# Product-key expert kernel on one core: the first head's expert lookup in three pieces, and the lookups of the later heads dealt one behind the other

## The reference

```python
q = einsum('bnd,de->bne', layernorm(x), w_q)                  # 512 -> 2 halves * 8 heads * 128
q = (q - mean(q, (0,1))) * rsqrt(var(q, (0,1)) + eps) * gamma + beta
sim = einsum('pbnhd,hkpd->pbnhk', q, keys)                    # 2 halves, 8 heads, 128 keys
sx, ix = top_k(sim[0], 8);  sy, iy = top_k(sim[1], 8)
scores, pk = top_k(sx[..., :, None] + sy[..., None, :], 8)    # best 8 of 64 pairs
idx = take(ix * 128 + iy, pk)                                 # 8 experts per token and head
h = gelu(einsum('bnd,bnhkd->bnhk', layernorm(x), down[idx])) * softmax(scores)
out = x + einsum('bnhk,bnhkd->bnd', h, up[idx])
```

## Time and profile before

| quantity | value |
|---|---|
| median of 3 runs | 2746.43 us (2737.4 to 2747.01) |
| the profiled execution | 2732.75 us, span 2730.9 us |
| PE, DVE, ACT, POOL busy | 86%, 68%, 43%, 42% of the span |
| rows fetched by POOL's queue | 469.82 MB |
| mean granted TensorE clock | 0.943 |

### The profile page before, as it was taken

How to read it: one execution, slowest core, us unless ns; L and a number is a source line. 1 busy time by engine, 2 the same in 40 slices (tenths; PEclk the granted TensorE clock), 3 DMA queues, 4 the chain that set the end, 5 groups by cost and what they waited for, 6 DMA issues and landing times.

```text
span 2730.9 us, 37792 instructions
## 1 busy us (share of the span) xinstructions
PE 2356.3 (86%) x12444; PEld 1259.1 (46%) x12444; DVE 1869.2 (68%) x5474; ACT 1176.5 (43%) x3224; POOL 1144.1 (42%) x1082
## 2 busy tenths in 40 slices
PE   8999999999999999998868888778878788876767
PEld 4565555656555565655534433333333343332323
DVE  4676777777687777768467767677775766766554
ACT  3365574736557473657223423323333332332222
POOL 3111212111121211120166576676667666577665
PEclk9999999999999999999989999989899998898889
DMA  4001001010100101011189899999999999899998
GB/s 175 30 1 37 8 8 37 1 44 1 41 4 10 36 1 43 1 60 58 58 320 364 299 369 357 349 354 345 358 352 363 351 362 358 309 359 356 355 375 330
DMA packets 161954, 521.78 MB, mean 191 GB/s; under 512 B 17248, under 2 KB 27488, under 8 KB 161760
## 3 DMA queue, kind: packets, MB, share of 16 engines
q0 software_dynamic: 129024, 469.82, 45.8%
q1 hardware_dynamic: 31152, 48.03, 5.3%
q10 hardware_dynamic: 1584, 1.52, 0.2%
HBM read 508.30 MB, written 11.01 MB: 190 GB/s over the span
## 4 chain that ended last, share of the span: by engine, by line
PE 20%; issue 10%; DVE 10%; another core or an unknown queue 3%; POOL 3%; DMA 3%; ACT 1%; DVEq 1%; POOLq 0%; ACTq 0%
PE ps_y L1819 7%; PE ps_o L1819 7%; DVE e_rows L1965 5%; PE ps_s L1789 3%; POOL e_rows L1769 3%; DMA e_rows<-in_experts,e_idx 3%; PE ps_t L1802 1%; ACT e_diag L2047 1%; DVE acc L1955 1%; DVE e_at L1899 1%; DVE e_best_at L1879 1%; DVEq L1903 0%; DVE q_stats L1847 0%; ACT e_q_t L2022 0%
## 5 line engine op out<-in xcount | busy, mean ns | idle before, releaser
L1769 POOL DMA_INDIRECT e_rows<-in_experts,e_idx x896 | 908.6, 1014 | 473.0 <-issue 284.6
L1965 DVE CUSTOM_DVE_ANT_0 e_rows<-e_rows,xn_all 128x512 f32<-128x512 f32 x896 | 568.6, 688 | 148.4 <-DMA e_rows<-in_experts,e_idx 112.5
L1819 PE MATMUL ps_o<-e_rows,e_diag 128*128 128x512 f32 x896 | 443.1, 642 | 149.2 <-issue 131.3
L1819 PE MATMUL ps_y<-e_rows,e_diag 128*128 128x512 f32 x896 | 434.5, 632 | 121.6 <-ACT e_diag L2047 60.4
L2047 ACT ACTIVATE e_diag<-ident_f,e_weight 128x128 f32<-128x128 f32 x896 | 286.3, 390 | 560.5 <-DVE e_weight L1976 197.1
L1819 PEld LDWEIGHTS ps_o<-e_rows,e_diag 128*128 128x128 f32 x896 | 179.8, 206 | 384.7 <-issue 362.5
L1819 PEld LDWEIGHTS ps_y<-e_rows,e_diag 128*128 128x128 f32 x896 | 178.1, 203 | 355.1 <-issue 316.1
L1133 DVE SCALAR_TENSOR_TENSOR ring<-ps_s,mask 112x750 f32<-112x750 f32 x248 | 225.0, 936 | 129.2 <-PE ps_s L624 110.1
L1359 ACT ACTIVATE ring<-ring,neg_max 112x750 f32<-112x750 f32 x248 | 226.8, 916 | 157.6 <-DVE neg_max L1143 157.2
L1143 DVE CUSTOM_DVE_ANT_0 ring<-ring,mask_bias 112x750 f32<-112x750 f32 x248 | 233.5, 989 | 0.0
L2042 ACT ACTIVATE e_active<-e_hidden 128x4 f32<-128x4 f32 x224 | 45.6, 204 | 359.5 <-DVE e_hidden L1965 143.3
(11 more groups left out here) (226 smaller groups left out, 3189.8 us busy)
## 6 DMA issues: line engine op xcount, KB each, us to landing
e_rows<-in_experts,e_idx POOLq DMA_INDIRECT x896
xn_t<-in_ctx_t SPq DMA_DIRECT2D x8, 1500.0 KB, 6.7
w_in<-in_ffn_wq SPq DMA_DIRECT2D x16, 256.0 KB, 7.6
acc<-in_x SPq DMA_DIRECT2D x8, 448.0 KB, 4.9
acc<-x_dram SPq DMA_DIRECT2D x7, 512.0 KB, 6.5
xn_all<-x2n_dram SPq DMA_DIRECT2D x7, 512.0 KB, 7.1
out<-acc SPq DMA_DIRECT2D x14, 256.0 KB
x_dram<-x SPq DMA_DIRECT2D x7, 448.0 KB, 3.1
```

Source lines behind the costliest of these rows:

```text
L1769: pool.indirect_dma_start(rows[:, v % RING, k, :], None, table[:, :], bass.IndirectOffsetOnAxis(ap=idx[:, e:e + 1], axis=0))\
L1819: mm = nc.tensor.matmul(ps_out[t % 2][:], diag[:, HU * (v % ND) + k, :], rows[:, v % RING, k, D:], start=(s == 0 and k == 0), stop=(s == S ...
L1965: last = nc.vector.tensor_tensor_reduce(down, down, xn_all[:, t, :], 1.0, 0.0, ALU.mult, ALU.add, hidden[:, b, k:k + 1])
```

## The change

1. **Seam.** The last transposes of the attention write to `cross_bank(last, t)` (ps_y, ps_o) in place of `ps_t[t]`. The freed `ps_t[0]` takes a new `second_project`: the first column of head 0, half 1, on TensorE between `turn_last(1)` and `first_project(3, ...)`.
2. **Head 0 in `first_head`.** The other three columns of half 1 go first, then all seven matches of half 0, which now write to the four `ps_q` banks and wait for no search, then only the three first matches of half 1. Half 1's query uses the banks ps_m[0], ps_m[1], ps_out[0], ps_out[1]. ScalarE's `affine` waits per column for the matches that read the part of `q_t` it overwrites. The projections of head 1 no longer stand here.
3. **Three pieces** (0, 2), (2, 6), (6, 14). The first two are searched, paired and chosen ahead of the units. The last one, eight tiles, goes into steps of the units 0 to 5 (`REST_PE`, `REST_DVE`, `REST_ACT`, `FIRST_REST`).
4. **Dealing.** The steps of head 1 go two per unit into the units 1 to 20 of head 0. Those of each later head go evenly, 40 steps over 28 units, from v = 21 of the head two before to v = 20 of the head before. No two heads' steps overlap any more.

```diff
+            def second_project():
+
+                pe.wait_ge(act_ready.sem, act_ready.at(last, 3 * NT))
+                for kc in range(KC):
+                    mm = nc.tensor.matmul(ps_t[0][:, 0:QN], w_in[:, (KC + kc) * P:(KC + kc + 1) * P], xn_t[:, kc, 0:QN],
+                                          start=(kc == 0), stop=(kc == KC - 1))
+                mm.then_inc(second_q_done, 1)
...
             turn_last(1)
+            second_project()
             first_project(3, 0)
...
-FIRST_TILES = 2
-PIECES = ((0, FIRST_TILES), (FIRST_TILES, NTF))
+PIECES = ((0, 2), (2, 6), (6, NTF))
...
             if head == 0 and half == 1:
-                return (ps_out[0], ps_out[1], ps_q[0], ps_q[1])[c]
+                return (ps_m[0], ps_m[1], ps_out[0], ps_out[1])[c]
...
+        def sims_out(head, half, g):
+
+            if head == 0 and half == 0:
+                return ps_q[g // 2][:, (g % 2) * TPB * NK:(g % 2 + 1) * TPB * NK]
+            return ps_m[g % 2][:, 0:TPB * NK]
...
-        LEAD = 20
-        AHEAD = 2 * QC
-        FIRST_TURNS = [0, *(min(N_STEPS, AHEAD + 2 + 3 * v // 2) for v in range(NV))]
-        SECOND_TURNS = [0, 1, 2, 3, 4, 5, 6, 7, 8, 10, 12, 13, 14, 15, 16, 17, 18, 20]
-        SECOND_AT = NV - len(SECOND_TURNS) + 1
+        LAST_AT = 20
+
+        REST = PIECES[-1]
+        REST_PE = {0: [("match", 1, 3), ("match", 1, 4)], 3: [("match", 1, 5), ("match", 1, 6)]}
+        REST_DVE = {0: [("search", 0, 3), ("search", 0, 4)], 1: [("search", 0, 5), ("search", 0, 6)],
+                    2: [("search", 1, 3), ("search", 1, 4)], 3: [("search", 1, 5), ("search", 1, 6)],
+                    4: [("pairs", 0, 0), ("pairs", 0, 1)], 5: [("pairs", 0, 2), ("pairs", 0, 3)],
+                    6: [("choice", 0, 0), ("choice", 0, 1)], 7: [("choice", 0, 2), ("choice", 0, 3), ("choice", 0, 4)]}
+        REST_ACT = {5: [("soften", 0, 0)]}
+        FIRST_REST = ((0,), (1,), (2,), (3,), (4, 5), (6, 7))
...
+        START_AT = 1
+
+        def unit_of(head, k):
+
+            if head == 1:
+                return START_AT + k // 2
+            return NV * (head - 1) - (NV - LAST_AT) + 1 + k * NV // N_STEPS
...
         def steps_in(h, v):
...
+            return DEAL.get(NV * h + v, ())
...
             def first_head():
 
-                group_at = {1: (0, 1), 2: (2, 3), 3: (4, 5, 6)}
-                for c in range(QC):
-                    for part in range(2):
-                        project(0, 1, 2 * c + part)
-                    for g in group_at.get(c, ()):
-                        match_keys(0, 0, g)
-                ahead_at = {2: (0, 1, 2, 3, 4), 4: (5,), 5: (6,), 6: (7,)}
+                for i in range(2, 2 * QC):
+                    project(0, 1, i)
                 for g in range(NG):
+                    match_keys(0, 0, g)
+                for g in range(REST[0] // TPB):
                     match_keys(0, 1, g)
-                    for i in ahead_at.get(g, ()):
-                        project(1, 0, i)
...
-                for g in range(NG):
-                    search(0, 0, g)
-                    if 1 <= g <= QC:
-                        count(0, 1, g - 1)
+                for c in range(QC):
+                    count(0, 1, c)
                 affine(0, 1)
                 dve.wait_ge(iota_ready, 1)
-                done = 0
-                for n0, n1 in PIECES:
-                    for g in range(done, n1 // TPB):
-                        search(0, 1, g)
-                    done = n1 // TPB
+                for n0, n1 in PIECES[:-1]:
+                    for half in range(2):
+                        for g in range(n0 // TPB, n1 // TPB):
+                            search(0, half, g)
...
-                if n >= 1:
-                    act.wait_ge(sims_made, NG * n)
                 for c in range(QC):
+                    if n >= 1:
+                        act.wait_ge(sims_made, NG * (n - 1) + min(NG, -(-QN * (c + 1) // (P * TPB))))
```

More of the change, by code:

```diff
@@ L1435, in last_cross @@
                     n = last * S + t * TT
-                    nc.scalar.copy(xn_t[:, :, n:n + TT], ps_t[t][:, 0:KC * TT].rearrange("p (c n) -> p c n", c=KC))\
+                    nc.scalar.copy(xn_t[:, :, n:n + TT], cross_bank(last, t)[:, 0:KC * TT].rearrange("p (c n) -> p c n", c=KC))\
                         .then_inc(last_t_ready, 1)
@@ L1642, in q_bank, with sims_needed, first_searched @@
             if head == 0 and half == 1:
-                return (ps_out[0], ps_out[1], ps_q[0], ps_q[1])[c]
+                return (ps_m[0], ps_m[1], ps_out[0], ps_out[1])[c]
             return ps_q[c]
+        def sims_out(head, half, g):
+            if head == 0 and half == 0:
+                return ps_q[g // 2][:, (g % 2) * TPB * NK:(g % 2 + 1) * TPB * NK]
+            return ps_m[g % 2][:, 0:TPB * NK]
+        def sims_needed(head, half, g):
+            if head == 0 and half == 0:
+                return min(g // 2 * 2 + 2, NG)
+            return NG * nth(head, half) + g + 1
+        FIRST_SEARCHES = [(half, g) for n0, n1 in PIECES for half in range(2) for g in range(n0 // TPB, n1 // TPB)]
+        def first_searched(half, g):
+            return FIRST_SEARCHES.index((half, g)) + 1
         def piece_of(n0, n1):
@@ L1806, in steps @@
             def steps(head, k):
-                for stage, half, part in PE_STEPS.get(k, ()):
-                    if head == 1 and k < AHEAD:
-                        continue
+                for stage, half, part in steps_of(PE_STEPS, REST_PE, head, k):
                     (project if stage == "project" else match_keys)(head, half, part)
@@ L1937, in steps @@
             def steps(head, k):
-                for stage, half, part in DVE_STEPS.get(k, ()):
+                n0, n1 = REST if head == 0 else (0, NTF)
+                for stage, half, part in steps_of(DVE_STEPS, REST_DVE, head, k):
                     if stage == "count":
@@ L1945, in steps @@
                     elif stage == "pairs":
-                        pairs(head, part)
+                        pairs(head, part, n0, n1)
                     else:
-                        choice(head, part)
+                        choice(head, part, n0, n1)
             def add_rows(h, t):
```

62 lines of the change are left out of this document (32 added, 30 removed).

## The result

The changed kernel takes 2783.72 us (median of 4 runs, 2775.65 to 2790.21) against 2743.36 us: a ratio of 1.0148, 95% interval 1.0113 to 1.0183. It is slower by 40 us: less than 2%, but clear of the noise, and outside the range of the prediction (2700 to 2757). The profiled execution is the one of 2775.65 us, 42.9 us above that of before.

What follows compares the result with a forecast made beforehand. The prediction took the gather's transfers to bound the expert part. Gains of 5.2 (first index), 8.4 (hole) and 4 us (end of head 0), dealing 0, sum to 17.6 us; subtracted from the median, 2729 us, range 2700 to 2757.

Steps and rivals of the forecast that it cites:

- that is the pace of the gather: Head 7: its units, 5.70 us each at a DMA share of 0.97, were taken to show the gather's pace.
- rival 4: Start: first index comes no earlier and a new wait replaces the hole; 2746 us, chance 0.06.
- Seam and first index: Start: expert part begins 2.4 us later, yet head 0's first gather comes 5.2 us earlier, at 1353.0.
- The hole: Head 0's start: POOL's 12.37 us wait for the second piece's indices goes, regaining 8.4 us of transfer.
- Is it too thin?: Head 0, units 0 to 10: DMA starves about 2 us, ring reserve gone some 40 us; 3 us charged.
- rival 2: Head 0: two steps per unit and one 10 us stall leave 4 us of the gain; 2743 us, chance 0.20.
- The end of head 0: Head 0's last stretch, DMA share 0.70 for 40 us: 7 of 12 us regained, 4 us net after a charge.
- Dealing 0: Heads 1 to 6: the even deal changes nothing, 0 us; bounds 24 us gained or 32 us lost.
- rival 3: Pairs and choice, squeezed into fewer units, cost 4.5 us more in each of seven heads; 2761 us, chance 0.14.

Runs made afterwards that it cites:

- before_again: The kernel before, unchanged, run again for its trace; ratio 1.0008 to the kernel before.
- changed_third: The changed kernel, unchanged, run once more in one session with its parts; ratio 1.0054 to the kernel before.
- changed_again: The changed kernel, unchanged, run once more; ratio 1.0116 to the kernel before.
- pieces_alone: The kernel before with head 0's tiles in three pieces, all ahead of the units, nothing else moved; ratio 1.0021 to the kernel before.
- seam_only: The changed kernel with the third piece's lookup and head 1's projections ahead of the units, and the old deal; ratio 1.0004 to the kernel before.
- choice_spread: The kernel before with heads 2 to 7 dealt evenly, but pairs and choice one step per unit (v = 13 to 20); ratio 1.0067 to the kernel before.
- deal_alone_again: The kernel before with only the steps of heads 2 to 7 dealt evenly, 40 over 28 units; ratio 1.0046 to the kernel before.
- projects_ahead: The changed kernel with the old deal from head 3 on and head 1's eight projections of half 0 ahead of the units; ratio 0.9993 to the kernel before.

## Why the prediction was wrong, point by point

The step that failed is the first one, "that is the pace of the gather", read from the DMA share of 0.97 in head 7, with what it put at nothing on that strength: engine work inside the units. It gave the even deal 0, and head 0's extra steps 2 us of starved DMA and a charge of 3. Measured in the result: 29.8 us in heads 1 to 6 and 2.0 in head 7, and a head 0 that is 35.2 us longer, against units that begin 27.9 us earlier.

At level A half the bytes change nothing and a quarter fewer issues give 140 us, so heads 1 to 6 go near the pace of POOL's issues (112 x 1.30 = 146 us a head, measured 148 to 150) and head 0 near TensorE's. The prediction had the number in hand, 1.27 us from issue to issue, and set it aside as "under the 1.43 us a gather takes", a figure that was itself only head 7's time divided by its issues. A high DMA share did not tell which of the two was the bound. That the result was slower had been given a chance of 0.14. (In that sum, half of rival 4's 0.06 stands under "faster", although its 2746 is no change.)

Neither half the bytes nor fewer issues were tried at level B, and there heads of 166 to 172 us are not at the pace of the issues either. The timeline of POOL reads: in before 832 of the 895 steps from one issue's start to the next are of 2 us or less and sum to 1101.0 us, and 63 longer ones to 255.2; in after 810 sum to 1063.9 and 85 to 337.1. (At level A before_again has 22 longer ones with 61.2 us, changed_third 32 with 99.8.) So the 42.9 us of span are: first issue -7.3, issues' steps -37.1 + 81.9 = +44.8, and 5.4 behind the last issue. The loss is in POOL's long waits, most of them for TensorE to free a ring unit, and not in slower issues.

*Seam and first index: right.* Forecast 1353.0, measured 1350.95, 1354.31 (changed_again) and 1351.47 (changed_third): against 1358.23 (before), 1358.28 (pieces_alone, set 2) and 1358.96 (before_again): 4 to 7.5 us earlier.

*The hole: it closes, and another opens.* The 8.4 us were counted as transfer regained. Without a wait for an index the ring of six units is full after 24 issues, and POOL waits for the engines instead: 9.13 us at unit 7 in after, 22.56 us at unit 6 in pieces_alone, 10.87 us at unit 6 in seam_only. Neither of those two runs beats the kernel before. Rows that come earlier wait in the ring for engines that are not ready for them. That a closed hole is worth nothing in every order of the lookup is not shown: in pieces_alone the units also begin 9.5 us later.

*"Is it too thin?": right sign, size wrong.* I charged 2 us and a share of 3. TensorE inside head 0 carries the projections that stood ahead of the units before (8 x 1.50 = 12 us), in the time that the "hole" had given it for nothing, and it was at 141 of 147.8 us already. Units 1 to 5 also carry steps of head 0 and of head 1 side by side, so the change's description, that no two heads' steps overlap any more, is true only of the later heads. At level A head 0 takes 172.1 us in the changed kernel against 147.8, and begins 22.2 us earlier: head 1 starts 2.1 us later. TensorE is busy for 9.6 us more in it and VectorE for 9.8, so some 15 of the 24.3 us are time in which TensorE stands. At level B it takes 198.5 us against 163.3, and 16.6 us of that are the longer step from unit 0 to unit 1. Its signs were the ones that the prediction had named for rival 2, a POOL wait of over 5 us in units 6 to 16 (9.13 and 5.93).

*"The end of head 0": wrong.* The window of 0.70 is still there, 0.72 with TensorE busy for 41.70 of 46.50 us: the stretch was mostly TensorE's. That steps moved elsewhere in the same head cannot shorten it is argued.

*Dealing 0: wrong; rival 3 was nearest.* At level A it costs 0.46%, 12 us or 2 us a head. In the result heads 1 to 7 take 31.8 us more, and rival 3 had 32. That this agrees so closely is partly luck: rival 3 put the cost down to the density of pairs and choice, and choice_spread, which spreads them, is still 17 us slower than before. The windows of v = 15 to 18, 18 to 20 and 20 to 24 of head 4, of before_again and then of deal_alone_again, show where:

```profile
2064.41:2083.04 18.63, 13.52 (x27) 5.18 (x25) 17.40 (x47) 10.08 (x21) 14.66 (x14) 0.91 1.00 381
2083.04:2090.21 7.17, 6.15 (x14) 2.69 (x15) 6.70 (x24) 5.31 (x14) 5.65 (x6) 1.00 1.02 389
2090.21:2111.31 21.10, 21.10 (x64) 10.73 (x63) 15.37 (x59) 5.93 (x20) 16.03 (x17) 1.00 1.02 402
```

```profile
2068.20:2089.48 21.28, 14.28 (x29) 5.77 (x27) 18.86 (x81) 7.32 (x18) 16.71 (x16) 0.90 1.03 409
2089.48:2098.48 9.00, 8.28 (x13) 3.67 (x14) 8.67 (x26) 2.97 (x10) 6.90 (x7) 0.65 1.01 384
2098.48:2117.01 18.53, 18.53 (x46) 8.55 (x45) 12.79 (x41) 5.93 (x20) 14.23 (x15) 1.00 1.01 398
```

v = 15 to 20 take 30.3 us in place of 25.8 (29.3 to 31.1 in heads 1 to 6, against 25.6 to 26.1). The even deal puts two parts of pairs or choice into one unit twice, and those two steps from weights to weights take 8.7 and 8.5 us on average, against 6.8 and 6.0; 2.6 of the 4.5 us come back in the third row. In v = 18 to 20 (second row) TensorE is granted 0.65 of its clock here and 0.81 in most heads, where the old deal has 0.76 in three heads and 1.00 in three. Which share is the clock's and which VectorE's was not measured by itself. Two readings speak against taking this stretch for the whole cost. With half the bytes it is as long (29.2 to 30.8 us against 26.2 to 27.4), and yet heads 1 to 6 lose nothing. And in choice_spread three of six heads have it at 24.5 to 24.7 us, with a clock of 1.00 in v = 18 to 20 of all six, and the kernel is slower all the same. How the even deal costs its time stays open.

*What level B adds.* There VectorE has 33 idle times of 4 us or more in the expert part of each kernel, 191.6 us in before and 220.6 in after; at level A 2 (before_again) and 4 (changed_third). Rival 2's "one stall of 10 us" is this, and it was two stalls of 8.94 and 6.67 us at the point where the ring could not help. What stops the engines there was not shown. No operand was late; ScalarE, too, begins unit 1's gelu after 7.17 us for which the profile shows no cause, while TensorE works on until 1378.2 and only then waits, for ScalarE. The runs with half the gather fell on level A, which has none of these stops. That the engines lack instructions while the gathers fill the queues is argued only.

The Trainium skill, "SBUF — State Buffer", section "SBUF: two separate sides", says that GpSimd cannot write the descriptors of its DMAs while VectorE runs an instruction in a mode that takes the port pair they share. The issues do not show it: one takes 1.014 us on average in before and 1.007 in after (0.999 in before_again, 1.000 in changed_third), so the moved lookup did not slow them. Whether the lookup's instructions run in such a mode no run shows.

## What to carry to other kernels

A DMA share near 1.0 does not say that transfers set the pace. Look at the engine that issues them too, whose busy row leaves out the gap between two issues, and multiply the issues by the step from start to start (896 x 1.30 us here). Work taken out of an idle time ahead of a loop and put into its first rounds costs nearly its full length if the engine that does it is the bound there (11.4 us of work and 10.3 us of time in projects_ahead). So cost a head's rounds by each engine's busy sum before calling a hole a loss, and after closing a hole look where the next wait stands. Halving the bytes of a transfer, then cutting its issues, are two small edits that tell which of the two a kernel pays for; the results are then other ones.

## What the hardware showed that was not expected

- An indirect DMA of 128 rows costs POOL 1.03 us with rows of 2 KB and 1.00 us with 4 KB, and 0.30 us pass before the next.
- One kernel ran at two levels 6% apart, 2584 to 2587 us (A) against 2743 to 2752 (B), at granted clocks of some 0.977 and 0.943. Its first gather is issued at the same moment at both (1358.96 and 1358.23 us), and heads 1 to 6 take 893.3 and 1010.2 us: the difference arises only in the part that gathers rows. What makes the level is not known.
- At level A VectorE has 2 idle times of 4 us or more in that part of the kernel before, at level B 33. The one between units 0 and 1 comes in each trace of the changed kernel and its variant at level B (21.1, 21.8 and 23.2 us from weights to weights), and in none at level A (4.7 to 4.8 us).
